# Moving the cut parts of q and k into the attention operand rows by copies within SBUF

## The reference, cut to what matters

```
q = rotary(Wq @ layernorm(x) + bq);  k = rotary(Wk @ ctx + bk);  v = Wv @ ctx + bv
scores = einsum('bdhn,bdhm->bhnm', q, k) / sqrt(8)
prob = softmax(scores, axis=-1)
x = x + Wm @ einsum('bhnm,bdhm->bdhn', prob, v) + bm
```

## Time and profile before

| what | us |
|---|---|
| median of the runs | 691.25 |
| lowest run | 683.17 |
| the profiled execution, its own time | 690.62 |
| span of its profile | 688.9 |

### The profile page before, as it was taken

How to read it: one execution, slowest core, us unless ns; L and a number is a source line. 1 busy time by engine, 2 the same in 40 slices (tenths; PEclk the granted TensorE clock), 3 DMA queues, 4 the chain that set the end, 5 groups by cost and what they waited for, 6 DMA issues and landing times.

```text
span 688.9 us, 12080 instructions
## 1 busy us (share of the span) xinstructions
PE 482.5 (70%) x3519; PEld 368.4 (53%) x3519; DVE 384.4 (56%) x1235; ACT 221.6 (32%) x578; POOL 349.4 (51%) x476
## 2 busy tenths in 40 slices
PE   0741898888898430699989994157764499999960
PEld 0630344444443210688877783145553499999950
DVE  8981576788786460154444442689955044444426
ACT  0451065555667310333323331134431122222210
POOL 9394221115556673256545537014444867777730
PEclk9985599888899655799999998597765599999985
DMA  5089989746588697789999723961111799999927
GB/s 184 4 203 244 341 291 298 218 94 155 166 238 279 208 402 285 229 270 313 347 298 309 244 95 106 353 273 55 70 69 61 258 388 360 349 353 361 375 100 276
DMA packets 82915, 163.95 MB, mean 238 GB/s; under 512 B 13070, under 2 KB 58142, under 8 KB 81072
## 3 DMA queue, kind: packets, MB, share of 16 engines
q1 hardware_dynamic: 56832, 106.20, 46.3%
q0 software_dynamic: 13968, 32.29, 12.7%
q10 hardware_dynamic: 12064, 24.84, 12.4%
HBM read 104.94 MB, written 66.78 MB: 249 GB/s over the span
## 4 chain that ended last, share of the span: by engine, by line
PE 32%; DMA 13%; DVE 9%; issue 2%; POOL 2%; ACT 1%; SPq 1%; POOLq 0%; DVEq 0%
PE sc_ps L1790 11%; DMA hd_side<-held 6%; PE hd_ps_up L1246 6%; PE sc_ps L1772 5%; DMA rows<-hd_side_out,hd_side_target 3%; PE hd_ps_out L1252 2%; DMA sc_rows<-rows 2%; PE hd_ps_x L1224 2%; PE sc_ps L1780 1%; DVE sc_rows L1879 1%; PE sc_ps L1740 1%; POOL rows L1393 1%; PE sc_ps L1728 1%; DVE sc_n_stats L1473 1%; DMA listed<-sc_empty,sc_index 1%
## 5 line engine op out<-in xcount | busy, mean ns | idle before, releaser
L1021 DVE TENSOR_REDUCE at_top<-at_ps_top 128x2 f32<-128x512 f32 x128 | 83.2, 685 | 46.4 <-PE at_ps_top L926 45.6
L1393 POOL DMA_INDIRECT rows<-hd_out,hd_rows x64 | 62.2, 972 | 59.3 <-DVE hd_out L1344 36.9
L1093 ACT ACTIVATE at_prob<-at_ps_score 128x512 f32<-128x512 f32 x128 | 72.6, 594 | 51.2 <-PE at_ps_score L944 50.6
L926 PE MATMUL at_ps_top<-e_arena 96*128 96x256 bf16 x256 | 57.6, 315 | 37.2 <-PEq L107 21.9
L1246 PE MATMUL hd_ps_up<-hd_x_turned,e_arena 128*128 128x160 f32 x512 | 82.7, 305 | 0.0
L1790 PEld LDWEIGHTS sc_ps<-sc_t_turned,e_w 128*112 128x112 f32 x672 | 80.6, 180 | 2.6
L1790 PE MATMUL sc_ps<-sc_t_turned,e_w 128*112 128x128 f32 x672 | 82.0, 276 | 0.0
L1246 PEld LDWEIGHTS hd_ps_up<-hd_x_turned,e_arena 128*128 128x128 f32 x512 | 76.1, 192 | 8.7 <-issue 6.2
L682 POOL DMA_INDIRECT held<-e_extended,e_address x64 | 62.4, 975 | 28.4 <-issue 17.7
L682 POOL DMA_INDIRECT listed<-e_extended,e_address x32 | 33.6, 1049 | 69.0 <-DVE e_address L674 61.5
L1381 DVE TENSOR_TENSOR hd_inner<-hd_silu,hd_ps_up 128x160 f32<-128x160 f32 x64 | 20.5, 321 | 81.8 <-ACT hd_silu L1331 81.8
(11 more groups left out here) (266 smaller groups left out, 911.6 us busy)
## 6 DMA issues: line engine op xcount, KB each, us to landing
e_w<-in_weights SPq DMA_DIRECT2D x42, 704.0 KB, 6.0
e_arena<-in_weights SPq DMA_DIRECT2D x52, 384.0 KB, 11.4
held<-e_empty ACTq DMA_DIRECT2D x16, 960.0 KB, 7.2
hd_rows<-held SPq DMA_DIRECT2D x15, 768.0 KB, 10.5
sc_rows<-rows SPq DMA_DIRECT2D x8, 1024.0 KB, 13.8
sc_tile_rows<-listed SPq DMA_DIRECT2D x42, 144.0 KB
parts<-op_parts SPq DMA_DIRECT2D x8, 576.0 KB, 6.7
e_arena<-in_weights ACTq DMA_DIRECT2D x12, 384.0 KB, 4.0
```

The lines of the kernel that those rows point to most:

```text
L926: last = nc.tensor.matmul(ps_top[at % TOPS][:, half, :], q_in[n][0:TOP, columns(at, half)], k_in[n][0:TOP, columns(at)], start=True, stop= ...
L1021: nc.vector.reduce_max(top[:, 2 * h:2 * h + 2], ps_top[at % TOPS][:], AX_X).then_inc(top_found, 1)
L1093: nc.scalar.activation(prob[at % RING][:], ps_score[at % SCORES][:], ACT.Exp, scale=scale).then_inc(prob_ready, 1)
L1393: nc.gpsimd.indirect_dma_start(rows_out, to, out_ap, None, bounds_check=TOKENS * LAYER0.chosen - 1, oob_is_err=False).then_inc(semaphore, 16)
```

## The change

The parts no longer go by DRAM: `load` now issues twelve transfers for a batch, six for q and six for k, each of which copies one slot of `parts` (128 partitions by 256 columns, 64 KB) into 8 operand rows. Since k's slots are used three, two and one time, the copies are 3 + 2 + 1 for k. The stores and their semaphores are gone; ACT's cut of batch 4 and later waits for the twelve copies of the batch four before. SP issues the copies of the batches 0 to 3 in the projection block, and those of the batches 4 to 7 in the attention block, in place of ACT and at the same step. POOL's memsets of the rows are gone; SP fills rows 48 to 98 of k (51 rows, 408 KB) and rows 48 to 95 of q (48 rows, 384 KB) of the four buffers from a constant in DRAM, behind the loads of the inputs. PE waits for all eight fills before its first score.

```diff
-    LOADS = PARTS + 1
+    Q_LOADS, K_LOADS = TERMS, PARTS * (PARTS + 1) // 2
+    LOADS = Q_LOADS + K_LOADS
...
-    def set_rows(self, nc, pool, n):
-
-        nc.gpsimd.memset(self.k[n][0:TOP].bitcast(F32), 0.0)
-        nc.gpsimd.memset(self.q[n][0:TOP].bitcast(F32), 0.0).then_inc(self.rows_set, 1)
-        pool.wait_ge(self.rows_set, 2 * n + 1)
-        nc.gpsimd.memset(self.k[n][TOP:ROWS].bitcast(F32), ONES_PAIR).then_inc(self.rows_set, 1)
-        pool.wait_ge(self.rows_set, 2 * n + 2)
+    def fill(self, engine):
+
+        for n in range(DEEP):
+            engine.dma_start(self.k[n][STACK:ROWS, :].bitcast(F32), self.fill_dram).then_inc(self.filled, 16)
+            engine.dma_start(self.q[n][STACK:TOP, :].bitcast(F32), self.fill_dram[0:TOP - STACK]).then_inc(self.filled, 16)
 
     def load(self, engine, b):
-        n = b % DEEP
-        if b < DEEP:
-            engine.wait_ge(self.rows_set, 2 * (b + 1))
-        engine.wait_ge(self.stored[b % self.OUT], 16 * (b // self.OUT + 1))
-        q_from = self.parts_dram[b, 0:TERMS].rearrange("t (d h) n -> (t d) (h n)", h=H)
-        engine.dma_start(self.q[n][0:STACK, :], q_from).then_inc(self.loaded[n], 16)
+        n, parts = b % DEEP, self.parts[b % self.OUT]
+        for t in range(TERMS):
+            to = self.q[n][t * HD:(t + 1) * HD, :].rearrange("d (h n) -> d h n", h=H)
+            engine.dma_start(to, parts[:, t, :]).then_inc(self.loaded[n], 16)
         row = 0
         for i in range(PARTS):
-
-            m = PARTS - i
-            k_from = self.parts_dram[b, TERMS:TERMS + m].rearrange("t (d h) n -> (t d) (h n)", h=H)
-            engine.dma_start(self.k[n][row:row + m * HD, :], k_from).then_inc(self.loaded[n], 16)
-            row += m * HD
+            for m in range(PARTS - i):
+                to = self.k[n][row:row + HD, :].rearrange("d (h n) -> d h n", h=H)
+                engine.dma_start(to, parts[:, TERMS + m, :]).then_inc(self.loaded[n], 16)
+                row += HD
...
             setup.sp_load(sp)
-            for b in range(B):
-                n = b % OUT
+            operands.fill(sp)
+            for b in range(DEEP):
                 sp.wait_ge(low_cut, b + 1)
-                sp.dma_start(parts_dram[b].rearrange("t p n -> p t n"), parts[n][:]).then_inc(stored[n], 16)
-                if 2 <= b < DEEP + 1:
-                    operands.load(sp, b - 2)
+                operands.load(sp, b)
...
-            for n in range(2):
-                operands.set_rows(nc, pool, n)
...
-                if b == 3:
-                    operands.set_rows(nc, pool, 2)
...
                 if b >= OUT:
-                    act.wait_ge(stored[b % OUT], 16 * (b // OUT))
+                    act.wait_ge(loaded[b % OUT], 16 * Operands.LOADS)
...
-            operands.load(sp, DEEP - 1)
...
+                b = batch_at(at, H + 4)
+                if b is not None and b + DEEP < B:
+                    sp.wait_ge(weighted, 4 * (b + 1))
+                    operands.load(sp, b + DEEP)
...
-            operands.set_rows(nc, pool, DEEP - 1)
...
+                if at == 0:
+                    pe.wait_ge(operands.filled, 16 * 2 * DEEP)
...
-                b = batch_at(at, H + 4)
-                if b is not None and b + DEEP < B:
-                    act.wait_ge(weighted, 4 * (b + 1))
-                    operands.load(act, b + DEEP)
```

More of the change, by code:

```diff
@@ L173, with __init__ @@
     FIRST, MIDDLE, LOW = slice(0, 7, 6), slice(3, 8, 4), slice(5, 9, 3)
-    LOADS = PARTS + 1
+    Q_LOADS, K_LOADS = TERMS, PARTS * (PARTS + 1) // 2
+    LOADS = Q_LOADS + K_LOADS
     OUT = 4
-    def __init__(self, s, parts_dram, arena):
-        self.parts_dram = parts_dram
+    def __init__(self, s, fill_dram, arena):
+        self.fill_dram = fill_dram
         halves = arena.bitcast(BF16)
@@ L183, in __init__ @@
         self.parts = [s.sbuf(f"parts{n}", [P, self.SLOTS, D], BF16) for n in range(self.OUT)]
[L184 removed]
         self.loaded = [s.sem(f"loaded{n}") for n in range(DEEP)]
[L186 to L202 removed]
+        self.filled = s.sem("filled")
+    def fill(self, engine):
+        for n in range(DEEP):
+            engine.dma_start(self.k[n][STACK:ROWS, :].bitcast(F32), self.fill_dram).then_inc(self.filled, 16)
+            engine.dma_start(self.q[n][STACK:TOP, :].bitcast(F32), self.fill_dram[0:TOP - STACK]).then_inc(self.filled, 16)
+    def load(self, engine, b):
+        n, parts = b % DEEP, self.parts[b % self.OUT]
+        for t in range(TERMS):
+            to = self.q[n][t * HD:(t + 1) * HD, :].rearrange("d (h n) -> d h n", h=H)
+            engine.dma_start(to, parts[:, t, :]).then_inc(self.loaded[n], 16)
         row = 0
         for i in range(PARTS):
[L206 to L209 removed]
+            for m in range(PARTS - i):
+                to = self.k[n][row:row + HD, :].rearrange("d (h n) -> d h n", h=H)
+                engine.dma_start(to, parts[:, TERMS + m, :]).then_inc(self.loaded[n], 16)
+                row += HD
 class Setup:
@@ L237, in project_phase @@
 def project_phase(nc, x, x_all, ctx, weights, biases, rotary, operands, held, *constants):
-    parts_dram, parts, stored = operands.parts_dram, operands.parts, operands.stored
+    parts, loaded = operands.parts, operands.loaded
     OUT = operands.OUT
@@ L1955, in _, with two_layers @@
                 nc.vector.tensor_tensor(x_all[:, b, :], rows[b][:, 0, :], x_all[:, b, :], ALU.add).then_inc(last_summed, 1)
-def two_layers(nc, x, ctx, ctx_turned, consts_f, more, weights, biases, rotary, merge_weights,
+def two_layers(nc, x, ctx, ctx_turned, consts_f, more, fill, weights, biases, rotary, merge_weights,
                merge_biases, gate0, weights0,
@@ L1962, in scratch @@
         return nc.dram_tensor(name, shape, dtype, kind="Internal").ap()
-    parts_dram = scratch("parts", [B, Operands.SLOTS, P, D], BF16)
     attended = scratch("attended", [B, EACH, P, D])
@@ L1980, in two_layers @@
                 space = Space(nc, attention, "op_")
-                operands, inputs = Operands(space, parts_dram, arena), MergeInputs(space, merge_weights, merge_biases, gate0)
+                operands, inputs = Operands(space, fill, arena), MergeInputs(space, merge_weights, merge_biases, gate0)
                 project_phase(nc, x, x_all, ctx, weights, biases, rotary, operands, held,
@@ L2034, in laid_out @@
         "more": more.astype(np.float32),
+        "fill": np.concatenate([np.zeros((TOP - STACK, H * D // 2)), np.full((PARTS, H * D // 2), ONES_PAIR)]).astype(np.float32),
         "weights": np.stack([w.T for w in (L0_xattn_Wq, L0_xattn_Wk, L0_xattn_Wv, L0_xattn_Wm)], axis=1),
```

## The result

The changed kernel takes 712.64 us (median) against 690.95 us for the kernel before on the same chip: a ratio of 1.034, interval 1.027 to 1.040. It is slower. Its profiled execution took 706.64 us (span 704.9), 16.0 more than that of before; other runs took 711.65 and 713.64, at a mean granted clock of PE of 0.828 and 0.827 against 0.835 (full speed is 1). That the clock made this difference is not shown. The ratio of each experiment is to runs of the kernel before that were made beside it (medians 688.0 to 689.1), so it isn't the quotient of the medians printed here.

The account below looks back on a forecast made before the run. Transfers were taken to set the projection block's end, with a chain from the attention block's start onward. The sum was 690.6 + 15.2 (later start) - 3.2 (attention block) = 702.6, say 703 us; range 680 to 737.

Parts of the forecast that it names:

- Start: Kernel start: without POOL's row memsets PE starts near 9.9 instead of 15.76, 5.8 us sooner; first cut tile ready at 27.5.
- Fill: Behind the inputs on SP: 51 rows go to three engines, 0.36 us a row, 80 rows, ending at 41 us.
- Copies: Projection block: 0.66 us a row, middle of 0.45 and 0.865; three late engines' 48 rows run from 41 to 72.7 us.
- The slower rival: Projection-block copies crowd on their few rows, 1.4 us each, deciding from about 0.95; total 737 us; chance 0.30.
- The faster rival: Projection-block copies keep pace with SP's issue, 0.42 to 0.59 us each; total 674 to 692, at 680; chance 0.28.
- End of the block: Projection block's end: landing 1.8, cuts 4.6, barrier 1.0, 7.4 us together; attention block starts at 80.1, 15.2 later.
- Attention block: Attention block: ACT freed of loads, SP given copy issues; credits 3.3 and 0.9, charge 1 us, net -3.2.
- The -3.3 for `at_out`: Attention block: ACT loses four loads, so PE's 3.3 us wait for at_out is credited.
- `place` behind the copies: Attention block: place queued behind 7.1 us of SP issues a batch just fits; 1 us charged.
- The sign that the prediction had named: Attention block: PE's L944 waits for at_top_rows growing from 4 to over 10 us would show place held behind the copies.

Follow-up runs that it names:

- e8_before_fill: Kernel before, with its POOL row memsets replaced by fill transfers from the constant (48 and 3 rows for k, 48 for q): 680.32 us, ratio 0.987.
- e13_copies_alone: Changed kernel without its fill; the memsets of the kernel before stay on POOL: 723.51 us, ratio 1.051.
- e1_fill16: Changed kernel with the 51-row k fill split into transfers of 48 and 3 rows: two runs, 706.62 and 712.88 us, no median or ratio.
- e4_fill16_stride: Changed kernel with the k fill split into 48 and 3 rows and each copy writing rows six apart: 691.75 us, ratio 1.003.
- e7_stride: Changed kernel, 51-row fill kept, with each copy writing rows six apart: 703.62 us, ratio 1.023.
- e2_spread: Changed kernel with SP issuing the attention block's q copies behind place and k copies behind the next place: 706.28 us, ratio 1.027.
- e5_act: Changed kernel with the copies of batches 4 to 7 issued by ACT instead of SP, at the same step: 725.16 us, ratio 1.054.

## Why the prediction was right, and where it was not

The prediction said 703 us, with 0.49 for slower, 0.43 for no change and 0.08 for faster; the 703 itself lay a little under the 705 from which it counted a time as slower. The median is 712.64 and the profiled execution 706.64. Set against that execution, the sum was 4.0 us short: 0.6 too much at the block's start, 3.5 too little in the attention block, 1.1 too little in the rest. The 6.0 us between that execution and the median were left out by taking the two as one, which had been true of the kernel before to within 0.7.

**Start: right.** 5.8 us were forecast; PE started 6.75 sooner and the first copy came 6.45 before the first store had. The first normalisation took 2.68 instead of 6.13 us, so POOL's memsets had held it. Removal shows it too: PE starts at 9.00 in e8_before_fill, and with the memsets back at 15.76 (e13_copies_alone).

**Fill: right, and shown by removal.** The transfer share from 20 to 40 us is 0.23, against three engines' 3/16 = 0.19 with the first copies on top. The forecast end was 41 us; SP came free at 41.75, but the fill's own rows took longer: 16 of its packets of 8 KB start between 41.75 and 45 us, none after. That is some 0.41 us a row (33 us by the prediction's 80 rows, an estimate) where 0.36 was charged. That three engines carry it is worked out from the rows that divide and from this share; the trace doesn't name the engines. With 48 and 3 rows the hang is gone (e1_fill16, e4_fill16_stride), and with the 51 rows back it returns (e7_stride).

**Copies: right size, half of the reason.** 0.66 us was taken as the middle between packets without a crowd and the mean of the old load; 0.65 was measured, and the last issue came at 71.3 where 72.7 was forecast. The crowd is real: 1.07 us a copy when nothing breaks it (e1_fill16, e13_copies_alone). That the fill's late engines thin it was argued, and the two-by-two table agrees. But what set the 0.65 is SP's issue, which stayed at 3.89 us for six with packets of 36 ns and with packets of 28. The transfers themselves were only a little quicker, 107 GB/s or 0.61 us a copy from 50 to 64 us. So the start came out right by some luck: the middle of two bounds fell on the price of an issue, the fill ended some 4 us later than forecast, and what followed was 42 issues of about 0.65 us behind SP's release, not 48 rows of 0.66 on the late engines. The prediction knew an issue price, 0.59 from `place`, and used it for the attention block alone. Had the packets been shorter, its forecast for this block would have been too early.

**The slower rival** lived inside the forecast. Its mechanism holds at 1.07 us instead of 1.4, a little above the 0.95 from which it was said to decide, and was held off by the slow fill. The Trainium skill's page "SBUF — State Buffer" (section "Door 1: The DMA port swizzle") has eight neighbouring rows on two ports, which makes 54 GB/s and 1.2 us for a copy by its figure, an estimate. The trace agrees with the rule in kind and comes out faster, 61 GB/s. By the formula in the same section of the Trainium skill's page, rows six apart lie on six or seven ports, an estimate. The trace agrees: there the crowd is gone (28 ns a packet).

**The faster rival** needed the fill spread or over in time, short packets and 0.42 to 0.59 us an issue. With the first two given (e4_fill16_stride) the issue cost 0.65, and the block started at 66.1, not at 55 to 63. The 674 to 692 us stated for this rival don't follow from its own terms: 690.6 less 2 to 10 and less 4.2 is 676 to 684.

**End of the block: right.** 7.4 us were charged from the last issue to the first score; it took 8.2, because the landing took 2.5 instead of 1.8.

**Attention block: the step that failed.** The -3.3 for `at_out` was measured as such (4.5 to 1.2). `place` behind the copies was charged with 1 us, because 7.1 us of issues, at the 0.59 us of a `place`, seemed to fit between the load and the next `place`. In batch 4 the twelve issues took 15.5 us, and PE's wait for `place` in the whole block grew by 10.1, nearly all of it there. The sign that the prediction had named, waits for `at_top_rows` from 4 to over 10 us, is there. Yet the block grew by only 0.3, not by 10.1 - 3.3. The windows of the block, of the kernel before and of the changed one (columns as in the earlier trace rows), have most of the difference:

```profile
64.86:275.03 210.17, 148.57 (x1185) 74.54 (x1185) 138.29 (x360) 93.14 (x200) 93.17 (x179) 0.78 0.79 250
79.46:289.95 210.49, 143.42 (x1185) 71.32 (x1185) 138.03 (x360) 93.07 (x200) 88.03 (x176) 0.80 0.74 243
```

PE's 1185 instructions took 5.2 us less, at a mean granted clock of 0.80 instead of 0.78, and its waits for DVE's maxima fell from 15.1 to 13.0 us. With these, 10.1 - 3.3 - 5.2 - 2.1 is -0.5, near the 0.3 measured. The prediction had neither term, and why the granted clock came out higher was not tried. So its error of 3.5 us for the block is smaller than that of the term for `place`, which other terms hid. e2_spread shows the same from the other side: 9.8 us of the wait for `place` were taken away, the wait for DVE's maxima grew by 11.8, and the block kept its length. So the term that was mis-sized is not `place` as such but SP's time; whatever stands behind the copies in SP's program, `place` or the packed rows, comes late.

One thing stays open. The issues of batch 4 cost 1.28 us each on SP also with rows six apart (8.12 and 7.25 us for six in e4_fill16_stride), but 0.74 on ACT (4.98 and 3.89 in e5_act), in a stretch in which the fill of the empty rows uses the transfer engines too. The two don't compare engine with engine: while SP issues, ACT goes on issuing empty rows (at 117.36, 120.59 and 123.70 in the changed kernel, transfer share 1.02 and then 0.82 in SP's two stretches), but while ACT issues the copies it issues none until 126.78, and the share is 0.85 and then 0.62. What SP's queue waits for there was not tried.

## What to carry to other kernels

Here a transfer within the chip cost its issuer 0.65 us for each copy and crowded on the rows that it wrote: count the copies by the issue price, spread one copy's rows, and give a transfer a row count that divides over 16 engines. When a change has two parts, time each alone, since here one part alone (the fill, split) made the kernel 1.3% faster and the other alone 5% slower; and when removing one cause makes things worse, look for a second that it was hiding. A wait that is taken off one engine is a gain only if nothing else stands behind the place where its work goes. Before a wait is set against a time, look at how long the engine's own instructions took.

## What the runs showed of the hardware that was not expected

- A copy of 64 KB into eight neighbouring rows ran at 61 to 62 GB/s (82 ns for a packet of 512 bytes), into rows six apart with 28 ns, the packet time of a store to DRAM from 128 rows.
- The issue of one such copy occupies SP for 0.65 us (3.89 for six) where nothing holds it, with packets of 36 ns as with packets of 28, more than the 0.59 of a `place` of 16 pieces.
- Behind a fill of 51 rows, which by the row count leaves three transfer engines late, neighbouring-row copies were faster than behind one of 48 + 3 (107 against 61 GB/s from 50 to 64 us) and the block started earlier (79.46 against 85.50). That the lag is the reason is inferred.
- The same 1185 instructions of PE in the attention block took 140.7 to 148.6 us from kernel to kernel, at mean granted clocks of 0.77 to 0.82.
